# The loop over six images of an attention stage written out, on all five engines

## What is computed

```python
def reference(x, Wq, bq, Wk, bk, Wv, bv, weight, bias, mask_weight, filter):
    # x: (8, 512, 32, 32); _gn: group norm over 32 groups of channels
    x = x + _L0_conv_ref(_gn(x), Wq, bq, Wk, bk, Wv, bv)      # attention
    x = x + _L1_conv_ref(_gn(x), weight, bias, mask_weight, filter, 1)
    return x

def _L0_conv_ref(x, Wq, bq, Wk, bk, Wv, bv):
    t = x.reshape(B, C, S).transpose(0, 2, 1)                 # S = 1024 tokens
    q, k, v = t @ Wq.T + bq, t @ Wk.T + bk, t @ Wv.T + bv
    q, k, v = (a.reshape(B * 8, S, 64) for a in (q, k, v))    # a plain reshape
    attn = softmax(einsum('gqd,gkd->gqk', q, k) / sqrt(64))
    wv = einsum('gqk,gkd->gqd', attn, v)
    return wv.reshape(B, S, 8, 64).transpose(0, 2, 3, 1).reshape(B, C, W, H)

def _L1_conv_ref(x, weight, bias, mask_weight, filter, padding):
    x_relu = maximum(x * _get_mask(x, mask_weight, filter), 0)
    return conv_general_dilated(x_relu, weight, 3x3, padding 1) + bias
```

## Time and profile before

| | |
|---|---|
| Time, median of three runs | 2628.54 us (2628.47 to 2631.73) |
| The profiled execution | 2624.4 us |
| Its span, first to last instruction | 2622.4 us |
| Mean granted clock of TensorE | 0.993 |
| Busy: PE, DVE, ACT, POOL | 94%, 74%, 44%, 42% |
| HBM traffic | 95 GB/s over the span |

### The profile page before, as it was taken

One profiled execution on the slowest core, in us unless ns is written; L12 is line 12 of the kernel. 1 busy time (PEld: TensorE's weight loads), 2 busy tenths in 40 slices (PEclk: granted clock), 3 DMA queues, 4 the chain that ended last, 5 costly groups with the idle time before them and its releaser, 6 DMA issues.

```text
span 2622.4 us, 43917 instructions
## 1 busy us (share of the span) xinstructions
PE 2457.1 (94%) x13768; PEld 912.8 (35%) x13768; DVE 1934.6 (74%) x2645; ACT 1149.1 (44%) x2059; POOL 1097.6 (42%) x970
## 2 busy tenths in 40 slices
PE   6899899989989999998999999998999999999999
PEld 2233233323323333332333333332344444444444
DVE  5787778768768877877877788986766966967515
ACT  4455455545545555554564555457332132132100
POOL 1465466546546645653664665565103012021000
PEclk9999999999999999999999999999999999999999
DMA  3213222131322213132221323223443644633534
GB/s 125 75 47 85 72 80 81 43 97 47 88 73 86 72 42 104 40 88 90 69 81 33 103 71 104 73 67 101 153 143 135 242 150 150 245 133 141 192 99 174
DMA packets 162830, 268.47 MB, mean 102 GB/s; under 512 B 80160, under 2 KB 80288, under 8 KB 162592
## 3 DMA queue, kind: packets, MB, share of 16 engines
q1 hardware_dynamic: 162320, 264.41, 31.3%
q10 hardware_dynamic: 272, 1.05, 0.1%
HBM read 195.54 MB, written 52.69 MB: 95 GB/s over the span
## 4 chain that ended last, share of the span: by engine, by line
PE 78%; DVE 11%; issue 5%; ACT 2%; DMA 2%; POOL 1%; DVEq 0%; SPq 0%; ACTq 0%; POOLq 0%
PE bank L845 28%; PE bank L750 14%; PE bank L724 12%; PE bank L675 11%; PE bank L685 6%; DVE nmax L1277 6%; PE bank L696 4%; DVE prob_sum L1270 2%; ACT prob L927 2%; PE bank L706 1%; DMA q_top<-shift 1%; DVE val L1289 1%; DVE bn L222 1%; PE bank L737 0%; DVE den_sb L1298 0%
## 5 line engine op out<-in xcount | busy, mean ns | idle before, releaser
L1277 DVE TENSOR_REDUCE nmax<-bank 128x1 f32<-128x512 f32 x1024 | 647.0, 680 | 268.7 <-PE bank L696 252.7
L927 ACT ACTIVATE prob<-bank 128x512 f32<-128x512 f32 x1024 | 560.9, 593 | 554.3 <-PE bank L724 554.3
L845 PE MATMUL bank<-v,u_slab 128*128 128x512 f16 x3456 | 746.9, 379 | 0.0
L1107 POOL TENSOR_TENSOR prob_sum<-prob_sum,prob 128x512 f32<-128x512 f32 x354 | 481.9, 1361 | 387.2 <-ACT prob L927 386.9
L750 PE MATMUL bank<-prob,val 128*64 128x512 f32 x2048 | 503.6, 612 | 11.4 <-issue 6.3
L845 PEld LDWEIGHTS bank<-v,u_slab 128*128 128x128 f16 x3456 | 338.1, 98 | 406.9 <-issue 0.8
L1270 DVE TENSOR_TENSOR prob_sum<-prob_sum,prob 128x512 f32<-128x512 f32 x354 | 333.4, 942 | 3.2 <-DVE val L1289 0.2
L696 PE MATMUL bank<-k_hi,q_hi 64*128 64x512 f16 x1024 | 200.6, 387 | 61.1 <-DVE nmax L1277 47.5
L724 PE MATMUL bank<-q_hi,k_hi 64*128 64x512 f16 x1024 | 197.6, 382 | 43.4 <-ACT prob L927 43.0
L750 PEld LDWEIGHTS bank<-prob,val 128*64 128x64 f32 x2048 | 126.7, 137 | 251.5 <-issue 212.2
L675 PE MATMUL bank<-xn_hi,w_hi 128*128 128x512 f16 x512 | 196.1, 383 | 7.8 <-DVE xn_lo L1254 7.8
(11 more groups left out here) (145 smaller groups left out, 2848.2 us busy)
## 6 DMA issues: line engine op xcount, KB each, us to landing
u_slab<-u_scratch SPq DMA_DIRECT2D x72, 1024.0 KB, 5.0
xs<-x SPq DMA_DIRECT2D x28, 1024.0 KB, 5.4
tile<-x_scratch SPq DMA_DIRECT2D x26, 1024.0 KB, 6.9
u_scratch<-u_w SPq DMA_DIRECT2D x96, 192.0 KB, 2.7
den_sb<-recip_scratch SPq DMA_DIRECT2D x128, 128.0 KB, 2.9
x_scratch<-xr SPq DMA_DIRECT2D x16, 1024.0 KB, 4.9
xr<-x SPq DMA_DIRECT2D x15, 1024.0 KB, 8.0
res<-x_scratch SPq DMA_DIRECT2D x14, 1024.0 KB, 8.8
```

The lines of the kernel that those rows point to most:

```text
L845: mm = pe.matmul(bank_at(pos, co)[:].rearrange("p (i n) -> p i n", i=2), slab[:, l, c, co * P:(co + 1) * P], image[v][:, 2 * c:2 * c + 2, ...
L927: act.activation(prob[:, (2 * u + e) % 8], sc_bank[bank_turn(s * 16 + 2 * u + e, 16 * HPI)[0]][:], ACT.Exp, scale=float(D) ** -0.5).then_i ...
L1107: nc.gpsimd.tensor_tensor(acc, in0, prob[:, (2 * kc + 1) % 8], ALU.add).then_inc(s1["sum1"], 1)
L1277: dve.tensor_reduce(nmax[:, seg, part:part + 1], src[:], AX.X, ALU.max, negate=True)\
```

## The change

On each engine the hardware loop becomes a loop of the program that writes the kernel, so that the six passes are issued one after another with `i` a number. `Count` loses its register form, and every `value()` becomes the plain number `n`. Of tensor instructions, waits and DMAs none is added, taken away or moved.

```diff
 class Count:
-    def __init__(self, per):
-        self.n, self.per, self.i, self.entry = 0, per, None, 0
-
-    def loop(self, i):
-        self.i, self.entry = i, self.n
-
-    def done(self, passes):
-        assert self.n - self.entry == self.per, (self.n - self.entry, self.per)
-        self.i, self.n = None, self.entry + self.per * passes
-
-    def value(self):
-        return self.n if self.i is None else self.i * self.per + self.n
+    def __init__(self):
+        self.n = 0
...
                 if ring.n >= ago:
-                    pe.wait_ge(s1["ring_free"], ring.value() + 3 - ago)
+                    pe.wait_ge(s1["ring_free"], ring.n + 3 - ago)
...
-            with pe.Fori(0, B - 2) as i:
-                ring.loop(i)
+            for i in range(B - 2):
                 for s in range(1, HPI):
                     slot(i, s)
                 slot(i + 1, 0)
-            ring.done(B - 2)
...
-                dve.wait_ge(s1["ring_full"], ring.value() + 1)
+                dve.wait_ge(s1["ring_full"], ring.n + 1)
...
-            with dve.Fori(0, B - 2) as i:
-                ring.loop(i)
-                step.loop(i)
+            for i in range(B - 2):
                 for s in range(1, HPI):
                     slot(i, s)
                 slot(i + 1, 0)
-            ring.done(B - 2)
-            step.done(B - 2)
```

More of the change, by code:

```diff
@@ L218, in sync @@
             def sync():
-                dve.wait_ge(signal, step.value())
+                dve.wait_ge(signal, step.n)
             def moments(k, half, src):
@@ L559, in _ @@
             slot(0, 0, prev=False)
-            with sp.Fori(0, B - 2) as i:
+            for i in range(B - 2):
                 for s in range(1, HPI):
@@ L636, in _ @@
         def _(pe):
-            ring = Count(PER_RING)
+            ring = Count()
             def take():
@@ L1061, in _ @@
             slot(0, 0, prev=False)
-            with act.Fori(0, B - 2) as i:
+            for i in range(B - 2):
                 for s in range(1, HPI):
@@ L1213, in _ @@
             slot(0, 0, prev=False)
-            with pool.Fori(0, B - 2) as i:
+            for i in range(B - 2):
                 for s in range(1, HPI):
@@ L1234, in _ @@
         def _(dve):
-            ring = Count(PER_RING)
-            step = Count(STAT_STEPS)
+            ring = Count()
+            step = Count()
             def item():
-                dve.wait_ge(s1["ring_full"], ring.value() + 1)
+                dve.wait_ge(s1["ring_full"], ring.n + 1)
                 src = v_ring[bank_turn(ring.n, PER_RING)[0]]
@@ L1243, in item @@
                 return src
-            step2 = Count(0)
+            step2 = Count()
             moments, aggregate, centre, finish = statistics(dve, s_stat, step, NC)
@@ L1279, in max_item @@
                 if m == 15:
-                    dve.wait_ge(s1["ring_free"], 2 + ring.value())
+                    dve.wait_ge(s1["ring_free"], 2 + ring.n)
                     dve.tensor_tensor(nmin[:, 0:SEG], nmax[:, :, 0], nmax[:, :, 1], ALU.min).then_inc(s1["min_done"], 1)
@@ L1319, in first_pair_stat @@
                 (centre2, finish2)[k](src, s1["ring_free"])
-            mstep = Count(0)
-            vstep = Count(0)
-            ystep = Count(0)
+            mstep = Count()
+            vstep = Count()
+            ystep = Count()
             def chain(ins):
```

## The result

2590.44 us (median of 4 runs, 2583.83 to 2597.18) against 2628.51 us for the kernel before, timed beside it (4 runs, 2625.31 to 2631.73). The ratio is 0.9855, with a 95% interval from 0.9827 to 0.9883: 1.45% faster, 38.1 us. The forecast was 2589.1 us with a range from 2581 to 2600.

What follows compares the result with a forecast made beforehand. The prediction took TensorE, busy 94% of the span, to bound the kernel through its instruction stream. Back edges 35.1, register operations 4.2 and the entry 0.1 sum to 39.4 us saved: 2589.1 us, range 2581 to 2600.

Steps and rivals of the forecast that it cites:

- Term 1: Five loop back edges, read from slot 0's to slot 2's transpose in images 1 to 5: removing them saves 35.1 us.
- The range of 21.5 to 37 us for five edges: Bounds for the back edges: TensorE's branches alone at their shortest, up to 7.4 us of its timeline five times.
- the branch is cheap, its time is the transfers of that moment: Rival: TensorE's pause is queue waiting or transfers and stays in straight code; 2623.8 us, chance 0.03.
- Term 2: Register operations in the other slots: 0.10 us in each of seven slots, six passes, 4.2 us saved; bounds nothing to 8.4.
- What was taken at nothing: DMAs closer together by 7 us per image: no cost; if the shift row came late, up to 5 us in all.
- One sign that I had named for "right": TensorE's granted clock would stay at 1.0 without a dip from the first slots to the end.
- The sign for the closer transfers: Slot 1 ending later, on the shift row, would show that DMAs moved closer together cost time.
- Missed fetches in straight code: Rival: written-out instruction blocks arrive late, 7.0 us a miss; one in six late gives 2666 us; chance 0.04.
- Only a part comes back: Rival: pauses go, but register relief is hidden or closer transfers cost time; 2593.5 to 2598.5 us, chance 0.12.

Runs made afterwards that it cites:

- e10_after: The written-out kernel of the change, unaltered, measured again beside later variants: 2588.47 us, ratio 0.9832 to the kernel before.
- e3_two: Kernel before with loops kept on all engines, but two images in a pass and three passes, leaving two back edges of five: 2607.36 us, ratio 0.9919.
- e1_pe_only: Kernel before with only TensorE's loop written out; VectorE, ScalarE, GpSimd and SyncE keep theirs: 2599.74 us, ratio 0.9889.
- e9_pe_act: Kernel before with TensorE's and ScalarE's loops written out; VectorE, GpSimd and SyncE keep theirs: 2596.30 us, ratio 0.9865.
- e2_others: Kernel before with TensorE's loop kept and the loops of SyncE, ScalarE, GpSimd and VectorE written out: 2619.59 us, ratio 0.9967.
- e12_cut5: Kernel before with loops kept, but the pass cut before slot 5, giving five passes and four back edges: 2597.78 us, ratio 0.9878.
- e4_cut: Kernel before with loops kept, but the pass cut before slot 4, giving five passes and four back edges: 2602.42 us, ratio 0.9905.
- e11_loop_early: Kernel before, loops kept, with slot 1's load of x issued early, between the halves of the sums' way through memory: 2624.48 us, ratio 0.9984.

## Why the prediction was right

**Term 1, the back edges: right in cause and size.** 35.1 us were forecast. The first profile shows 335.6 - 304.0 = 31.6, with the shift-row waits of images 2 and 3 in it. The second profile of the same kernel (e10_after), which had next to none of them in images 1 to 5, shows 298.0 and so 37.6 us, a little above the 37 that I had given as the most. Three edges fewer gave 22.0 us (e3_two). The low clock behind each edge went with the standstill.

**But not TensorE's alone.** I named the other engines' branches as short, and so they are, 0.04 to 0.06 us; what follows them isn't, as their code has to come as well. This step named too few engines. Of the 37.6 us over the edges, 32.9 come back with TensorE's loop alone (e1_pe_only), 4.4 more with ScalarE's (e9_pe_act), and 0.3 are left for the three others. ScalarE's share shows only once TensorE's edge is gone: e2_others got nothing there, and its 9.8 us lie, as far as its trace shows them, in the slots without an edge. The sum was safe, since the term was read from whole slots and not from TensorE's pauses.

**The price of an edge is not a constant.** The range of 21.5 to 37 us for five edges held for this place. At other slots an edge costs 0.4 to 3.7 us (e12_cut5, e4_cut). The rival "the branch is cheap, its time is the transfers of that moment" was wrong as put, for the pause doesn't come without the branch; but of the 7 us most are gone at places with fewer transfers, and the traces put the late second block down to them.

**Term 2, register operations: 4.2 us forecast, 2.2 found.** From slot 2's evacuation to slot 0's of the next image the loop took 160.36 us (360.53 to 520.89) and the written-out image 1 159.99 us (355.77 to 515.76), 0.37 less, times six. Slots 2 and 3 gave the 0.20 I had read; the error was to carry 0.10 to all seven. Slots 4 and 5 gave nothing (28.85 before, 28.87 after). Slot 0 gave 0.1 us (28.97 by the evacuations in e3_two where it has no edge, 28.87 after), but in images 1 to 5 that lies in the stretch of term 1. The term was inside the bounds, and small. That it is small rests on all engines losing theirs together: on four of them, or on TensorE alone, the same slots moved by 7.3 us down and 5.5 us up.

**What was taken at nothing: the DMAs.** The wait for the shift row, priced at up to 5 us, was not made by the change. It was there before (e11_loop_early) and comes and goes from run to run; in the first profile it and the low clock behind it took away some 6 us in images 2 and 3. The rest of what that profile lacks is outside the changed part: it started image 1 2.9 us later than the profile before (294.63 against 291.77, first exponentials), and images 6 and 7, which no part of the change touches, took 3.7 us more. The part from image 1 to 5 gained 33.6 us there, and 33.6 - 2.9 - 3.7 is the 27.0 of the spans. In e10_after that part gained 39.5 us.

One sign that I had named for "right" didn't come in the first profile, the granted clock at 1.0 without a dip. Behind the wait of image 2 it fell to its lower level (0.72 over 575 to 581 us), and again in image 6 (0.72 over 1572 to 1578) and image 7 (0.72 over 1766 to 1772), which the change doesn't touch. The sign for the closer transfers, slot 1 ending later on the shift row, did come, and misled: the wait isn't the change's.

**How much of the hit is luck.** The median came within 1.3 us of the forecast, closer than the method allows: executions of the kernel spread over 13 us, and two medians of it lie 2 us apart. Against e10_after term 1 was 2.5 us too small and term 2 2.0 us too large, and the two errors nearly cancel. The mechanism and the size of the edges are no luck.

**The rivals.** Missed fetches in straight code: none. No pause of TensorE above 2 us in images 1 to 5 has "issue" beside it; the only ones stand on the shift row. q8 carried 113 packets, 16 fewer than the 129 before. "Only a part comes back" didn't happen either.

## What to carry to other kernels

A hardware loop whose head has to be fetched again pays for it at every back edge, and not on the busiest engine alone; here 7 us an edge, against 0.21 us for a branch whose target was a few instructions back. Before writing it out, look where the edge lies and what the busy engine has queued ahead of it: cutting the pass at another slot (with one edge fewer, and one more image's slots written out) gave 32 us, where writing everything out gave 38 to 43. And where a small transfer on which the busy engine waits is issued just behind a large one in the same queue, change their order: that was worth 4 to 6 us here, in either form of the kernel.

## What I had not expected

- The cut before slot 5, with four edges on five engines, costs 0.4 to 0.7 us an edge in the trace, a tenth of the old place or less.
- With TensorE in its loop and the other four written out (e2_others), slot 3 takes 20.54 us and slot 7 21.04, faster than with no register operation anywhere (20.88 and 21.36), and with TensorE written out and the others in their loops (e1_pe_only) 21.3 and 21.8, slower than before (20.94 and 21.42). Fewer sequencer instructions on one engine can make a slot longer. Which order of events does it wasn't tried.
- Executions of the changed kernel differ by up to 13 us (2583.8 to 2597.2 us). In the slowest, part of it is the receipt of a 4 KB store that SyncE waits for, 3.2 us in image 2 of the slowest one against 1.4 in image 5 (1226.61 to 1228.03), with the shift row late behind the first and in time behind the second.
